# A gated attention layer with routed experts: a product goes from GpSimd to VectorE, and the attention step is put in another order

## The reference, cut to what matters

```python
def xattn(x, context, Wq, Wkv, null_kv, Wout, ln_scale, ln_bias):       # x: 32 batches of 256 rows x 256
    q = split_heads(x @ Wq) * DH ** -0.5                                # 16 heads of 64
    k, v = split_heads(context @ Wkv)                                   # 77 keys, and one null key ahead
    attn = softmax(q @ k^T); out = (attn @ v) @ Wout
    return (out - mean(out)) * rsqrt(var(out) + EPS) * ln_scale + ln_bias
def ffn(h):                                                             # 8192 rows, 32 experts, 8 picked
    aff = sigmoid(h @ Wr + br)
    top_v, top_i = top_k(aff, 8); top_w = top_v / (sum(top_v) + 1e-9)
    shared = (silu(h @ Wg_s + bg_s) * (h @ Wu_s + bu_s)) @ Wd_s + bd_s
    down_e = (silu(h @ Wg[e] + bg[e]) * (h @ Wu[e] + bu[e])) @ Wd[e] + bd[e]
    return shared + sum over picked e of top_w[e] * down_e
x = x + tanh(g_xattn) * xattn(layernorm(x), ctx, ...)
x = x + tanh(g_ffn) * ffn(layernorm(x), ...)
```

## Time and profile before

| what | value |
| --- | --- |
| median of 3 runs | 2115.65 us (2113.9 to 2118.12) |
| profiled execution | 2113.35 us, span 2111.6 us |
| TensorE busy | 1979.2 us, 94% of the span |
| VectorE busy | 1612.2 us, 76% |
| ScalarE busy | 1384.4 us, 66% |
| GpSimd busy | 1215.3 us, 58% |
| granted TensorE clock, mean | 0.979 |

### The profile page before, as it was taken

How to read it: one execution, slowest core, us unless ns; L and a number is a source line. 1 busy time by engine, 2 the same in 40 slices (tenths; PEclk the granted TensorE clock), 3 DMA queues, 4 the chain that set the end, 5 groups by cost and what they waited for, 6 DMA issues and landing times.

```text
span 2111.6 us, 43649 instructions
## 1 busy us (share of the span) xinstructions
PE 1979.2 (94%) x14658; PEld 1741.3 (82%) x14658; DVE 1612.2 (76%) x3739; ACT 1384.4 (66%) x3988; POOL 1215.3 (58%) x1316
## 2 busy tenths in 40 slices
PE   7999799999999999999996899999999999999995
PEld 7888588888888888888885688889898888888884
DVE  5544247777777777777776866668999999999996
ACT  2100278788888887888873367777777777777771
POOL 0000104777777777777777500017777777777775
PEclk9999889999999999999997999999999999999998
DMA  9553378776666666667776998999999999999998
GB/s 274 161 151 124 124 293 313 251 233 230 227 225 228 223 232 225 226 229 235 235 260 221 346 332 287 285 298 384 403 402 400 397 394 393 386 402 396 394 364 285
DMA packets 319570, 605.45 MB, mean 287 GB/s; under 512 B 87509, under 2 KB 191670, under 8 KB 319350
## 3 DMA queue, kind: packets, MB, share of 16 engines
q1 hardware_dynamic: 270198, 468.39, 63.6%
q0 software_dynamic: 49152, 134.28, 17.3%
HBM read 305.00 MB, written 297.53 MB: 285 GB/s over the span
## 4 chain that ended last, share of the span: by engine, by line
PE 25%; DMA 18%; POOL 16%; DVE 14%; issue 9%; ACT 4%; SPq 3%; POOLq 0%; DVEq 0%; ACTq 0%
POOL pages_dram L788 14%; DMA w_raw<-in_experts 13%; DMA pages_dram<-blank 4%; DVE parts L1806 4%; PE ring L1308 3%; PE ring L139 2%; PE xps L1903 2%; PE ring L140 2%; PE ring L141 2%; DVE up_ps L1857 2%; DVE hid_l L1863 2%; DVE w_l L1780 1%; DVE wq_l L1768 1%; PE gate_ps L139 1%; PE yps L139 1%
## 5 line engine op out<-in xcount | busy, mean ns | idle before, releaser
L1697 POOL DMA_INDIRECT parts<-results_dram,kept_index x512 | 517.6, 1011 | 381.4 <-DMA results_dram<-y 220.7
L788 POOL DMA_INDIRECT pages_dram<-rows,kept_index x512 | 530.0, 1035 | 159.7 <-issue 148.1
L864 ACT ACTIVATE exps<-sim,minus_max 128x78 f32<-128x78 f32 x1024 | 317.2, 355 | 40.0 <-DVE minus_max L980 39.9
L864 ACT ACTIVATION_READ_ACCUMULATOR exps<-sim,minus_max 128x1 f32 x1024 | 242.3, 237 | 0.0
L1718 ACT ACTIVATE w_h<-w_raw 128x768 fp32r<-128x768 f32 x159 | 133.9, 842 | 149.6 <-DMA w_raw<-in_experts 149.6
L1806 DVE SCALAR_TENSOR_TENSOR parts<-parts,kept_weight 128x256 f32<-128x256 f32 x448 | 213.5, 477 | 1.1
L139 PE MATMUL ring<-xnT_h,wq_h 128*128 128x256 f32 x512 | 157.9, 308 | 29.4 <-DVE outT_l L1124 27.9
L1903 PE MATMUL xps<-ident,xin 128*128 128x128 f32 x1272 | 167.0, 274 | 18.0 <-DVE wq_l L1768 8.4
L1780 DVE TENSOR_TENSOR w_l<-w_raw,w_h 128x768 fp32r<-128x768 f32 x159 | 151.7, 954 | 40.1 <-ACT w_h L1718 39.6
L139 PE MATMUL yps<-w_h,hid_h 128*128 128x256 f32 x636 | 179.5, 282 | 1.7 <-DVE hid_l L1863 1.4
L141 PE MATMUL yps<-w_l,hid_h 128*128 128x256 f32 x636 | 178.3, 280 | 0.0
(11 more groups left out here) (240 smaller groups left out, 6056.0 us busy)
## 6 DMA issues: line engine op xcount, KB each, us to landing
xin<-pages_dram SPq DMA_DIRECT2D x159, 512.0 KB, 10.3
results_dram<-y SPq DMA_DIRECT2D x159, 512.0 KB, 9.5
w_raw<-in_experts SPq DMA_DIRECT2D x159, 385.0 KB, 9.4
pages_dram<-blank SPq DMA_DIRECT2D x108, 512.0 KB
pages_dram<-blank SPq DMA_DIRECT2D x12, 1536.0 KB
keys_dram<-keys SPq DMA_DIRECT2D x16, 616.0 KB, 4.2
kT<-keys_dram SPq DMA_DIRECT2D x32, 308.0 KB, 4.0
v<-values_dram SPq DMA_DIRECT2D x32, 308.0 KB
```

Of the source, the lines that this page charges most:

```text
L788: pool.indirect_dma_start(dram["pages"], bass.IndirectOffsetOnAxis(ap=kept_index[:, at:at + 1].bitcast(U32), axis=0), buffer(batch)[:, k / ...
L864: last = act.activation(exps[u % 2][:, h, :], scores(u)[:, h % 2, h // 2, :], ACT.Exp, bias=minus_max[u][:, h:h + 1], accum_out=row_sum[u] ...
L1697: pool.indirect_dma_start(parts[slot(batch, t)][:, k, :], None, done, bass.IndirectOffsetOnAxis(ap=kept_index[:, at:at + 1].bitcast(U32), ...
```

## The change

On GpSimd the product `weigh` is gone and stands in VectorE's step for all batches; the bias add is first in GpSimd's step, and the scatters are cut into 5, 9 and 2. The tables that set the order and the bank of each piece are new, and the steps of TensorE, ScalarE, VectorE and SyncE follow them. No instruction of another kind is added.

```diff
-RING = ["X", "N2", "Oa", "T0a", "Ob", "T1a", "T0b", "T1b", "L", "PV0a", "PV0b", "Q0", "Q1", "T2a", "T2b", "T3a", "Q2", "T3b", "R",
-        "Q3", "PV1a", "PV1b"]
+RING = ["X", "Oa", "Ob", "N2", "T0a", "L", "Q0", "T1a", "Q1", "T0b", "T1b", "Q2", "R", "PV0a", "PV0b", "T2a", "T3a", "T3b",
+        "T2b", "Q3", "PV1a", "PV1b"]
+BANK = {"X": 2, "Oa": 3, "Ob": 3, "N2": 1, "T0a": 0, "L": 2, "Q0": 1, "T1a": 0, "Q1": 2, "T0b": 1, "T1b": 3, "Q2": 0,
+        "R": 3, "PV0a": 2, "PV0b": 3, "T2a": 0, "T3a": 1, "T3b": 2, "T2b": 0, "Q3": 1, "PV1a": 0, "PV1b": 2}
...
             fill_pages(b, 1)
-            if 3 <= b <= B + 1:
-                store_weights(b - 3)
+            if 0 <= b <= B - 1:
+                if b > 0:
+                    sp.wait_ge(biased, b)
+                sp.dma_start(x_res[:, :, :], x_tiles[b]).then_inc(res_loaded, 16)
             if 2 <= b <= B + 1:
...
+            if 3 <= b <= B + 1:
+                store_weights(b - 3)
+            fill_pages(b, 2)
             if 0 <= b <= B - 2:
                 sp.wait_ge(sim_full, UNITS * (b + 1))
                 load_keys(b + 1)
-            fill_pages(b, 2)
...
+            if 1 <= b < B:
+                add_bias(b, par, h)
             if scatters:
...
                 scatter(b, range(0, 5))
             if 1 <= b < B:
                 make_rstd(1, b - 1)
-            if 3 <= b < B:
-                weigh(b - 3)
...
             if scatters:
-                scatter(b, range(5, 8))
+                scatter(b, range(5, 14))
+            if 1 <= b < B:
+                make_rstd(2, b - 1)
+            if scatters:
+                scatter(b, range(14, 16))
...
-            if scatters:
-                scatter(b, range(8, 16))
...
+            if 1 <= b <= B:
+                dve.wait_ge(ring_full, nth(RING, "Ob", b))
+                statistics(1, lambda t: bank("Ob", b)[:, t * D:(t + 1) * D], b - 1)
             if b >= -1:
                 low("N2", b)
...
             if 1 <= b <= B:
                 centre(b)
+            if routes and b < B:
+                route("top", b, par, h)
+            if routes and b < B:
+                route("mask", b, par, h)
+            if here:
+                normalise(2, b)
+            if b == B:
+                next(dense)
+            if routes:
+                route("placed", b, par, h)
+            if b >= 3:
+                weigh(b - 3)
+            if b == B + 1:
+                sum_weights(b - 3)
+            if here:
+                normalise(3, b)
             if b >= -1:
                 low("PV0a", b)
```

More of the change, by code:

```diff
@@ L85 @@
 VSLOTS = 2
-RING = ["X", "N2", "Oa", "T0a", "Ob", "T1a", "T0b", "T1b", "L", "PV0a", "PV0b", "Q0", "Q1", "T2a", "T2b", "T3a", "Q2", "T3b", "R",
-        "Q3", "PV1a", "PV1b"]
-BANK = {"X": 2, "N2": 0, "Oa": 3, "T0a": 1, "Ob": 3, "T1a": 0, "T0b": 2, "T1b": 1, "L": 0, "PV0a": 2, "PV0b": 1, "Q0": 0, "Q1": 2,
-        "T2a": 3, "T2b": 0, "T3a": 2, "Q2": 1, "T3b": 2, "R": 3, "Q3": 0, "PV1a": 3, "PV1b": 1}
+RING = ["X", "Oa", "Ob", "N2", "T0a", "L", "Q0", "T1a", "Q1", "T0b", "T1b", "Q2", "R", "PV0a", "PV0b", "T2a", "T3a", "T3b",
+        "T2b", "Q3", "PV1a", "PV1b"]
+BANK = {"X": 2, "Oa": 3, "Ob": 3, "N2": 1, "T0a": 0, "L": 2, "Q0": 1, "T1a": 0, "Q1": 2, "T0b": 1, "T1b": 3, "Q2": 0,
+        "R": 3, "PV0a": 2, "PV0b": 3, "T2a": 0, "T3a": 1, "T3b": 2, "T2b": 0, "Q3": 1, "PV1a": 0, "PV1b": 2}
 NBANK = 4
-COPIED = ["X", "N2", "T0a", "T1a", "T0b", "T1b", "PV0a", "PV0b", "Q0", "Q1", "T2a", "T3a", "T2b", "Q2", "T3b", "Q3", "PV1a", "PV1b"]
+COPIED = ["X", "N2", "T0a", "Q0", "T1a", "T0b", "T1b", "Q1", "Q2", "PV0a", "T2a", "T3a", "T2b", "T3b", "PV0b", "Q3", "PV1a",
+        "PV1b"]
 SPLIT = ["X", "N2", "PV0a", "PV0b", "PV1a", "PV1b"]
@@ L1180, in step @@
             if here:
+                maximum(2, b)
+            if b >= 3:
+                scale_weights(b - 3)
+            if here:
                 normalise(1, b)
-            if b >= 4:
-                sum_weights(b - 4)
-            if 1 <= b <= B:
-                dve.wait_ge(ring_full, nth(RING, "Ob", b))
-                statistics(1, lambda t: bank("Ob", b)[:, t * D:(t + 1) * D], b - 1)
             if here:
@@ L1219, in step @@
             if routes:
-                route("placed", b, par, h)
                 route("opened", b, par, h)
@@ L1319, in output @@
                     pe.wait_ge(null_v_loaded, 32)
-                pe.wait_ge(ring_hi, nth(COPIED, f"T{2 * half + 1}b", b))
+                pe.wait_ge(ring_hi, nth(COPIED, ("T1b", "T3b")[half], b))
                 first = HP * "ab".index(name[3])
@@ L1368, in step @@
                 next(dense)
-            if here:
-                similarity(1, b)
-            output("Oa", b, par, h)
+            output("T0a", b, par, h)
             if here:
                 similarity(2, b)
-            output("T0a", b, par, h)
-            output("Ob", b, par, h)
-            output("T1a", b, par, h)
-            output("T0b", b, par, h)
-            output("T1b", b, par, h)
-            if here:
                 similarity(3, b)
@@ L1386, in step @@
                 next(dense)
-            output("PV0a", b, par, h)
-            output("PV0b", b, par, h)
             output("Q0", b, par, h)
+            output("T1a", b, par, h)
             output("Q1", b, par, h)
-            output("T2a", b, par, h)
-            output("T2b", b, par, h)
-            output("T3a", b, par, h)
+            output("T0b", b, par, h)
+            output("T1b", b, par, h)
             output("Q2", b, par, h)
-            output("T3b", b, par, h)
             output("R", b, par, h)
@@ L1399, in step @@
                 next(dense)
+            output("PV0a", b, par, h)
+            output("PV0b", b, par, h)
+            output("T2a", b, par, h)
+            output("T3a", b, par, h)
+            output("T3b", b, par, h)
+            output("T2b", b, par, h)
             output("Q3", b, par, h)
```

96 lines of the change are left out of this document (39 added, 57 removed).

## The result

| what | before | after |
| --- | --- | --- |
| median, us | 2115.8 (2113.9 to 2118.1, 4 runs) | 2049.1 (2048.1 to 2052.3, 4 runs) |
| ratio, 95% interval | | 0.9687 (0.967 to 0.9704) |
| profiled execution, span | 2113.35, 2111.6 | 2052.32, 2050.6 |
| VectorE, GpSimd busy | 1612.2, 1215.3 | 1644.8, 1169.6 |

The account below looks back on a forecast made before the run. A GpSimd-VectorE loop with TensorE hanging on it was taken as the bound. 28 steps falling from 27.19 to 25.6 us gain 44.5, less 4 at attention's end, 40.5 us: 2075 us, range 2061 to 2103.

Parts of the forecast that it names:

- The bound and the loop: Attention step of 27.19 us: GpSimd and VectorE wait for each other in a loop, with TensorE hanging on it.
- What goes from GpSimd: The product leaves, 1.24 us a step; GpSimd's own step falls from 26.4 to 25.3 us, and the loop opens.
- the way a piece restarts: GpSimd's scatters: how a piece starts again after other work was held worth up to 0.46 us.
- What comes to VectorE: The product adds 0.69 us a step; VectorE's work becomes 22.0 us, not the bound, with over 3 us of slack.
- TensorE's floor: TensorE's own step without its waits is 25.6 us; grouping scores saves nothing or 0.36, so 25.2 to 25.6.
- Waits that the order makes: New waits of T1b, T3a and T3b on TensorE give back 0.4 to 0.8 us a step; step taken as 25.6.
- the walk: One step of the new order traced with row durations; T1b's balance came to 7.6 against 7.8 us.
- Where attention ends: Step 32: N2 behind Oa and Ob loses 5 us, 1 comes back; net loss 4 us, bounds 0 and 6.
- The residual behind the dense round: End of attention, VectorE: the residual now follows a dense round, which was said to cost 1.7 us.
- The port collision: VectorE and GpSimd on the shared SBUF port beside normalisations or product: 0.7 us a step, 2089 to 2111; 16 in 100.
- T1b's bank: T1b waits for a late `centre`; slower from 1.45 us a step on, 2134 us at 2.1 us; 10 in 100.

Follow-up runs that it names:

- e_product: The kernel before with only the product of weights and matched keys moved to VectorE, behind the match of keys: 2099.2 us, ratio 0.9928.
- e_scatters: The kernel before with only GpSimd's scatters cut 2, 6, 8, so the first rstd comes three scatters sooner: 2128.3 us, ratio 1.0066.
- e_less_pe: The changed kernel without the third matmul of each of the queries' products, 16 matmuls a step: 2041.2 us, ratio 0.9651.
- e_no_product: The changed kernel with VectorE's product cut to a sixteenth of its elements: 2051.5 us, ratio 0.9713.
- e_both: The kernel before with the product on VectorE and scatters cut 2, 6, 8, all engines in the old order: 2063.2 us, ratio 0.9756.
- e_bias_back: The changed kernel with GpSimd's bias add back behind the first rstd: 2066.4 us, ratio 0.9776.
- e_split: The changed kernel with both score pairs parted, X between first and second, T0a between third and fourth: 2086.7 us, ratio 0.987.
- e_tail_sum: The changed kernel with N2 and the shared-weight splitting earlier at attention's end, and step 32's residual ahead of the second dense round: 2047.3 us, ratio 0.968.
- e_back: The changed kernel with the product back on GpSimd, between the nine scatters and the second rstd: 2069.7 us, ratio 0.9803.

## Why the prediction was right and wrong

**The bound and the loop: right.** The three waits that it read as a loop are gone, and `e_product` and `e_scatters` show that the loop was one: with half of it opened, the waits remain or move.

**What goes from GpSimd: right in kind, its size off.** GpSimd's own step was put at 25.3 us (25.1 to 25.6); `e_less_pe` has it at 24.30. Of the 2.1 us between 26.4 and 24.30 the product is 1.24. The rest is in the scatters: what the 16 of a step take above 0.96 us each adds to 1.21 us before (1.43 and 1.28 in the earlier trace rows, and one of 1.26 at 612.21) and to 0.34 in `e_less_pe`. I had taken it for the way a piece restarts, as a property of the cut. It is one of the phase between two engines (last section). The count of pieces was wrong as well: before, the 8 scatters of a step and the 5 of the next are one run of 13, so there were two pieces and not three. Had GpSimd's step been 25.3, it would have set the kernel's step, and the order's gain below 25.3 would not have shown. The room for `rstd` was also smaller than said: it was to be ready at about 10 us for a need at 15.7; it ends at 614.89 and `z` starts at 616.46, 1.6 us later.

**What comes to VectorE: right.** Forecast at 0.69 us and free; it measures 0.68, and `e_no_product` shows 0.50 of it free.

**TensorE's floor: the failed step.** "Either nothing of this is saved or all 0.36: the floor is 25.2 to 25.6." TensorE's own step is 24.74, 0.46 us under the lower end of that floor, and with it the step of 25.6 and the range fell; GpSimd's lower bound of 25.1, which would have held the step up, was too high as well. Two things were wrong with the floor. First, the old order's own step is 25.39 (`e_both`) and not 25.6. The step lost 1.79 us from the kernel before to `e_both`: 1.57 in the queries, 0.18 in the transposes of the probabilities, 0.04 in Oa and Ob. The prediction subtracted 1.41 for `outT_l` and 0.19 for `pT`; the second is no wait of the loop (it stands in `e_both` unchanged), and it was counted again in the 0.36. Second, the new order gives 0.65 where 0.36 was the most allowed. I counted the idle time ahead of a score's loads, but the neighbours of a score and the scores themselves take less in the new order: 0.31 in the scores, 0.22 in Oa and Ob, 0.21 in N2 and 0.11 in L, less 0.13 that the transposes of the probabilities take more and 0.07 elsewhere.

**Waits that the order makes: the walk was close, its price was not.** It said that T1b waits 0.1 to 0.3 us, T3a 0.2 and T3b 0.3. None of the three occurs in a steady step. The balance of 7.6 against 7.8 us was as tight as said: `z` ends at 617.33 and T1b's place in TensorE's queue comes 0.1 us later, and in `e_bias_back` 0.5 us more on VectorE make T1b wait 0.30. So nothing comes back of the 0.4 to 0.8 us that the prediction charged.

**Where attention ends: the mechanism was right, the size short.** `x2T_l` now comes behind Oa and Ob, and `gate_ps` starts 16.6 us after the last load of values (1065.88, 1049.3), before 10.9 (1130.54, 1119.6). I had 5 lost and 1 back; in this profile the start is 5.6 late, another 2.2 go in the first dense round at the lower clock (last section), 1.2 elsewhere, and nothing came back: 9.0 in all. In `e_no_product` and `e_split`, with the same end, `gate_ps` starts 13.8 and 13.7 us after the last load, and the loss is 4.1 in all; so the loss lies between 4 and 9 us. Part of that spread goes with the granted clock, for which the forecast had no term. The residual behind the dense round is not why (`e_tail_sum`, 0.6 us by the median, within the spread of both).

**Rivals.** The port collision left the normalisations: `probs` has a mean of 808 ns, before 982. It went to `divisor`, where the forecast counted nothing because it had the bias add beside maxima, and where it cost nothing. The Trainium skill, SBUF — State Buffer, "Who interferes with whom", states that a VectorE instruction with two SBUF inputs contends with a GpSimd instruction that reads SBUF. The trace of `e_bias_back` agrees: `weight`, with both inputs in SBUF, started 0.55 us behind the bias add and ended 0.08 after it. T1b's bank made no kernel slower than the one before: a lateness of 1.45 us a step would have been needed for that, and the largest in steady steps is 0.8, in `e_less_pe`.

## What to carry to other kernels

Before pricing a loop of waits, find what stands between its two ends: here the product alone gave 16 us, the early rstd alone cost 13, and the two together gave 52. Price a switch of TensorE between kinds of matmul from start to start (a pair against a lone one, the piece ahead of it against the same piece elsewhere), not by the idle time shown ahead of its load; and before a mean of a wait is called small, look whether it is one wait or many. When one profile of a short stretch is compared with another, look at the granted clock of both. When a reordered steady step has an odd last step, price that step by itself.

## What the runs showed of the hardware

The collision on the shared port also acts against GpSimd. Its `var_eps` on 128x2 elements takes 0.21 us at 601.75 and 0.64 at 613.46, beside VectorE's `probs` (613.24, 0.81 us), and ends with it (614.10 against 614.05):

```profile
613.24 0.81 DVE L987 TENSOR_TENSOR probs<-exps,row_inv 128x624 f32<-128x624 f32 x1
```

```profile
1048.00:1058.00 10.00, 8.16 (x72) 7.51 (x68) 7.43 (x15) 4.38 (x9) 7.71 (x10) 1.00 0.34 119
```

That stretch is not what sets the round's pace: `e_no_product`, `e_split` and `e_back` have a clock of 1.00 there too, and their rounds take 4.31, 4.26 and 4.08 us; the kernel before has 0.67 there, and 2.65 us. What goes with the pace in all fourteen profiles is TensorE's idle time right before the round: 2.35 to 2.94 us in the eight kernels with the new end, whose rounds take 4.08 to 4.86, and at most 0.79 in the six others, whose rounds take 2.65 to 2.67. No run changes that idle time alone.
